# Six places in a quad for a router's choice, and the first gather moved beside the last quad

## What is computed

```
x = x + tanh(g_xattn) * attention(layernorm(x), ctx, mask)      # one head, 77 keys
n = layernorm(x)
probs = softmax(n @ gate_w.T)                                   # 8 experts
g, m = top_k(probs.transpose, k=512)                            # per batch and expert
h = gelu(n[m] @ w1) @ w2                                        # 512 -> 2048 -> 512
x = x + tanh(g_ffn) * scatter_add(g * h)
```

## Time and profile before

| | us |
|---|---|
| median of 3 runs | 1548.4 (1545.95 to 1549.63) |
| the profiled execution | 1545.97, its span 1543.9 |
| TensorE busy | 1493.0 (97%) |
| VectorE, ScalarE, GpSimd busy | 1012.3, 721.4, 587.7 |
| first hidden product of expert 0 starts | 172.19 |
| first output product starts | 180.67 |

### The profile page before, as it was taken

The page is one execution under the profiler, slowest core; times in us unless marked ns, Lnnn a source line. Parts: engine busy times, 40 slices in busy tenths (PEclk is TensorE's granted clock), DMA queues, the critical chain, the costliest instruction groups (busy, mean ns, idle before and its releaser), DMA issues.

```text
span 1543.9 us, 20288 instructions
## 1 busy us (share of the span) xinstructions
PE 1493.0 (97%) x7329; PEld 1226.4 (79%) x7329; DVE 1012.3 (66%) x1716; ACT 721.4 (47%) x1270; POOL 587.7 (38%) x552
## 2 busy tenths in 40 slices
PE   6987899999999999999999999999999999999997
PEld 6755577888788888888888888888888888888886
DVE  2687776557866667676757676667667675766543
ACT  2244433455444454454445544445445444554532
POOL 2264655525434135314443244413541444323311
PEclk9999799999999999999999999999999999999999
DMA  7274633533324333244323432333324433442133
GB/s 232 77 241 157 216 103 116 138 120 92 109 83 89 102 83 115 64 102 103 105 87 82 110 110 83 82 101 91 108 70 96 110 94 98 82 110 82 42 76 76
DMA packets 101385, 163.37 MB, mean 106 GB/s; under 512 B 7411, under 2 KB 45315, under 8 KB 101285
## 3 DMA queue, kind: packets, MB, share of 16 engines
q1 hardware_dynamic: 86885, 128.50, 26.3%
q0 software_dynamic: 14400, 33.56, 11.6%
HBM read 128.48 MB, written 33.55 MB: 105 GB/s over the span
## 4 chain that ended last, share of the span: by engine, by line
PE 90%; DVE 6%; DMA 1%; ACT 1%; issue 1%; POOL 0%; SPq 0%; POOLq 0%; DVEq 0%
PE bank L1410 43%; PE bank L1296 34%; PE bank L1272 4%; PE bank L1587 2%; PE bank L565 1%; PE bank L589 1%; DVE atleast L972 1%; DMA x_s<-in_x 1%; DVE onehot L1470 1%; DVE x L839 1%; PE bank L406 1%; PE bank L1459 0%; DMA ctx_raw<-in_ctx 0%; PE bank L554 0%; PE bank L582 0%
## 5 line engine op out<-in xcount | busy, mean ns | idle before, releaser
L1410 PE MATMUL bank<-w2hl,hh 128*128 128x512 f32 x2024 | 628.6, 392 | 0.4 <-DVE hid_low L1288 0.4
L1296 PE MATMUL bank<-xo,whl 128*128 128x512 f32 x2352 | 541.8, 389 | 1.9 <-DVE mix L1360 1.9
L1296 PEld LDWEIGHTS bank<-xo,whl 128*128 128x128 f32 x2352 | 441.4, 188 | 94.4 <-DVE mix L1360 2.3
L1410 PEld LDWEIGHTS bank<-w2hl,hh 128*128 128x128 f32 x2024 | 375.9, 188 | 75.8 <-DVE hid_low L1288 0.8
L1410 PE MATMUL bank<-w2hl,hid_low 128*128 128x512 f32 x1012 | 394.0, 389 | 0.0
L1410 PEld LDWEIGHTS bank<-w2hl,hid_low 128*128 128x128 f32 x1012 | 190.0, 188 | 39.7
L1534 POOL DMA_INDIRECT layer_out<-y,slot_row x64 | 104.6, 1635 | 294.6 <-ACT y L1449 279.3
L1226 POOL TENSOR_TENSOR whl<-raw,whl 128x512 fp32r<-128x512 f32 x56 | 81.3, 1451 | 259.5 <-ACT whl L1189 259.5
L1257 DVE TENSOR_TENSOR w2hl<-raw,w2hl 128x512 fp32r<-128x512 f32 x213 | 146.0, 707 | 38.5 <-ACT w2hl L1252 38.5
L1252 ACT ACTIVATE w2hl<-raw 128x512 fp32r<-128x512 f32 x228 | 136.5, 624 | 63.4 <-DMA raw<-in_L_ffn_w 39.5
L1231 POOL TENSOR_TENSOR whl<-wsum,whl 128x512 fp32r<-128x512 f32 x56 | 73.9, 1320 | 183.5 <-ACT whl L1210 183.5
(11 more groups left out here) (231 smaller groups left out, 1783.9 us busy)
## 6 DMA issues: line engine op xcount, KB each, us to landing
raw<-in_L_ffn_w SPq DMA_DIRECT2D x228, 256.0 KB
raw<-in_L_ffn_w SPq DMA_DIRECT2D x72, 512.0 KB
x_s<-in_x SPq DMA_DIRECT2D x8, 1024.0 KB, 9.2
layer_out<-x SPq DMA_DIRECT2D x8, 1024.0 KB, 10.4
xn_rows<-xn SPq DMA_DIRECT2D x8, 1024.0 KB, 5.2
raw_k<-in_L_xattn_Wk SPq DMA_DIRECT2D x1, 1024.0 KB, 5.4
raw_q<-in_L_xattn_Wq SPq DMA_DIRECT2D x1, 1024.0 KB, 11.0
raw_v<-in_L_xattn_Wv SPq DMA_DIRECT2D x1, 1024.0 KB, 13.2
```

Of the source, the lines that this page charges most:

```text
L1296: last = pe.matmul(bk[:, :], whl[:, p % 2, part, 2 * w + k, :], xo[:, xpart, x, k, :], start=(not adds and k == 0 and part == HIGH and xpa ...
L1410: last = pe.matmul(Y_BANKS[c][:, :], high if hpart == HIGH else low[:, c * P:(c + 1) * P], w2hl[:, f % 4, part, :], start=(s == 0 and hpar ...
```

## The change

- A quad has six places in place of five (`PLACES`), and piece 0 is at place 2 of quad 4 (`FIRST_PLACE`), at the same point of that quad as before. On TensorE place 0 is now ahead of `route`, and place 1, which is new, behind the second weighing; on VectorE place 0 is where it was and place 1 stands between `router_in` and `weights_in`. Quad 5 so has pieces 4 to 9, quad 6 has 10 and 11 ahead of its weighings, the one-hots (12) ahead of `weigh` 2 on VectorE with the slots' product ahead of weighing 3 on TensorE, and the slots (13) ahead of `weigh` 3. Quad 7 has none.
- In quad 7 TensorE turns two blocks of gathered tokens ahead of weighing 3 and the other two behind it. VectorE's low part of w1 moves from behind quad 7 to ahead of its `weights_in`, and all four low parts of tokens stand ahead of the two last `logits_out` (before, the fourth stood behind them).
- ScalarE does the squares of the quad before (`square_x1`) ahead of `exps` in quads 5 and 6; in quad 7 all four stand behind `e_out`. The tokens' high parts stand ahead of the last quad's squares.
- GpSimd does, for quads 4 and 5, all four rows ahead of `first_deviations` of the quad after the next, and the gather stands ahead of the `deviations` of quad 6.

```diff
@@ -537,7 +537,7 @@
         VG_BANK, CHOICE_BANK = bank[5], bank[7]
 
 
-        CHOOSE_FROM, PLACES = QB, 5
+        CHOOSE_FROM, PLACES, FIRST_PLACE = QB, 6, 2
 
         def turn_bank(turn):
             return bank[T_BANKS[turn_at[turn] % 2]]
@@ -606,21 +606,28 @@
                 turn_e(pe, q)
                 if q + 1 < NQ:
                     score(pe, q + 1, Q - 1)
+                between(q, 0)
                 if q == 0:
                     wait_evacuated(pe, len(steps) - 1)
                 route(pe, q)
-                between(q, 0)
-                for i in range(Q - 1):
+                for i in range(2):
                     weigh_pe(pe, q, i)
                 between(q, 1)
+                weigh_pe(pe, q, 2)
+                between(q, 2)
+                if q == NQ - 1:
+                    for c in range(2):
+                        tokens_pe(pe, 0, c)
                 weigh_pe(pe, q, Q - 1)
-                between(q, 2)
+                between(q, 3)
                 for i in range(Q):
                     if q + 2 < NQ:
                         turn_x(pe, q + 2, i)
                     if i == 1:
-                        between(q, 3)
-                between(q, 4)
+                        between(q, 4)
+                between(q, 5)
+            for c in range(2, NC):
+                tokens_pe(pe, 0, c)
 
         def attention_act(act):
             def square(q, i):
@@ -673,14 +680,15 @@
             for q in range(NQ):
                 if q == NQ - 1:
                     w1_high_act(act, 0, 0, 0)
-                    for i in range(2):
+                elif q - 1 >= LATE:
+                    for i in range(Q):
                         square_x1(q - 1, i)
                 exps(q)
                 e_out(q)
                 if q == CHOOSE_FROM:
                     choice_act(act, 0)
-                if q - 1 >= LATE:
-                    for i in range(2 if q == NQ - 1 else 0, Q):
+                if q == NQ - 1:
+                    for i in range(Q):
                         square_x1(q - 1, i)
                 if LEAD <= q + 1 < NQ:
                     for i in range(Q):
@@ -688,6 +696,9 @@
                 if q + 2 < NQ:
                     for i in range(Q):
                         x_out(q + 2, i)
+
+            for c in range(NC):
+                first_tokens_act(act, c)
             for i in range(Q):
                 square_x1(NQ - 1, i)
 
@@ -761,14 +772,16 @@
                 if q >= 0:
                     deviations(q)
                     for i in range(Q):
-                        if i == Q // 2:
+                        if i == Q // 2 and q < LATE:
                             first_deviations(it + 1)
                         rows(q, i)
-
-
-            deviations(NQ - 2)
+                    if q >= LATE:
+                        first_deviations(it + 1)
+
+
             for c in range(NC):
                 gather_pool(pool, 0, 0, c)
+            deviations(NQ - 2)
             deviations(NQ - 1)
             for f in range(2):
                 w2_low_sub(pool, 0, 0, f)
@@ -865,16 +878,17 @@
             prep_out(dve, prep_dve, False, 1, own)
             for q in range(NQ):
                 softmax_in(q)
-                if q == NQ - 1:
-                    between(q, 0)
                 if q >= 2 and q - 2 != CHOOSE_FROM - 1:
                     logits_out(q - 2)
                 if 1 <= q <= LATE:
                     stats(q - 1, range(Q))
                     moments(q - 1)
+                between(q, 0)
                 if q + 1 < NQ:
-                    between(q, 0)
                     router_in(q + 1)
+                else:
+                    w1_low_part(dve, 0, 0, 0)
+                between(q, 1)
                 weights_in(q)
                 weigh(q, 0)
                 if q == CHOOSE_FROM:
@@ -883,22 +897,20 @@
                 weigh(q, 1)
                 if q == NQ - 1:
                     mean_out(q, slice(0, Q // 2))
-                between(q, 1)
+                between(q, 2)
                 weigh(q, 2)
-                between(q, 2)
+                between(q, 3)
                 weigh(q, 3)
                 if q == NQ - 1:
                     mean_out(q, slice(Q // 2, Q))
                 elif q >= LATE:
                     mean_out(q)
-                between(q, 3)
                 between(q, 4)
-            w1_low_part(dve, 0, 0, 0)
-            for c in range(NC - 1):
+                between(q, 5)
+            for c in range(NC):
                 split_tokens_dve(dve, 0, c)
             logits_out(NQ - 2)
             logits_out(NQ - 1)
-            split_tokens_dve(dve, 0, NC - 1)
 
         def attention_over(eng):
 
@@ -1051,11 +1063,8 @@
         def beside_attention(do):
 
             def between(q, place):
-                at = (q - CHOOSE_FROM) * PLACES + place - 1
-                if q == NQ - 1:
-                    for piece in ((N_PIECES, N_PIECES + 1) if place == 0 else ()):
-                        do(piece)
-                elif 0 <= at < N_PIECES:
+                at = (q - CHOOSE_FROM) * PLACES + place - FIRST_PLACE
+                if 0 <= at < N_PIECES + 2:
                     do(at)
             return between
 
@@ -1985,8 +1994,6 @@
             prep_out(act, prep_act, True, 0)
             attention_act(act)
 
-            for c in range(NC):
-                first_tokens_act(act, c)
             for f in range(2):
                 w2_high_act(act, 0, 0, f)
             w1_high_act(act, 0, 0, 1)
@@ -2034,8 +2041,6 @@
         def _(pe):
             prep_pe(pe, 0)
             attention_pe(pe, beside_attention(first_choice_pe(pe)))
-            for c in range(NC):
-                tokens_pe(pe, 0, c)
             hidden_pe(pe, 0, 0)
 
             pe.wait_ge(rinv_ready, NQ)
```

## The result

The change costs a little: 1552.98 us (median of 19 runs, 1550.74 to 1555.73) against 1548.4 us (19 runs, 1545.95 to 1553.97), a ratio of 1.0028 (95% interval 1.0020 to 1.0035). The profiled execution took 1551.53 us, with a span of 1549.5 us against 1543.9. TensorE's mean granted clock over the runs was 0.9863 of full speed, against 0.9887 in the runs of the kernel before that stand beside experiments 1 to 8.

What follows compares the result with a forecast made beforehand. TensorE, busy 1493.0 of 1543.9 us, was taken as the bound. 0 (quads 5, 6) + 0.6 (quad 7) - 0.2 (squares to output) + 2.4 (clock) - 0.3 = +2.5 on 1548.4, so 1550.9 us; range 1544.5 to 1554.

Steps and rivals of the forecast that it cites:

- rival B: Quad 6: clock falls before 151 us, so slots and weighing 3 run at half clock; +3.8, 1552.2 us; chance 0.16.
- Part 1: Quads 5 and 6: six places and an earlier choice, VectorE's added work balanced by filled waits; 0 us.
- hot comparison: VectorE's large comparison for the one-hots, now in quad 6: 2.28 us, forecast to end near 150 us.
- Part 2: Quad 7: two token blocks turned ahead of weighing 3, +1.0, less 0.4 for the slots' product; last weighing 0.6 us later.
- rival C: Quad 7: gathered tokens land late and hold weighing 3; at 2 us late, 1552.9 us; chance 0.07.
- Rival D: Quad 7: the pause is cut in two, so the clock stays at 2.4 GHz; 1544.5 us; chance 0.14.
- Part 3: From quad 7's last weighing through squares, logits and choice to output: -0.2 us, between -0.9 and +0.6.
- Rival E: Before output: the hidden products are the bound and start 2.6 us earlier, no clock penalty; 1545.8 us; chance 0.10.
- Part 4: Before output: TensorE waits 4 to 6 us, so output products start at 1.2 GHz; 2.35 us, bounds 0 and 3.0.
- the 0.3 wait: TensorE's wait of 0.3 us for a count of the second choice, forecast to go away.
- Rival A: At output start: the clock holds, so no 2.4 us cost; time given as 1548.6 us; chance 0.13.

Runs made afterwards that it cites:

- experiments 1 to 8: Follow-up kernels, some editing the changed kernel and some the kernel before; their medians run from 1548.88 to 1557.45 us.
- experiment 7: Changed kernel plus extra products that nobody reads, in TensorE's pauses in quad 6 and before output; 1549.11 us, 1.0005 of the kernel before.
- experiment 5: Kernel before with only the six places and the earlier choice; gather, tokens and the ScalarE and GpSimd orders unchanged; 1549.56 us, 1.0009.
- experiment 10: Changed kernel with two of quad 7's squares ahead of the token copies, and unread products in pauses of quads 4 to 7 and before output; 1545.55 us, 0.9986.
- experiment 9: Changed kernel with two of quad 7's four squares ahead of ScalarE's token copies, two behind; 1551.83 us, 1.0013 of the kernel before.
- experiment 3: Changed kernel with all four squares of quad 7 ahead of ScalarE's token copies; 1557.45 us, 1.0057 of the kernel before.
- experiment 4: Changed kernel with all four token blocks turned behind quad 7's last weighing; 1555.18 us, 1.0046 of the kernel before.
- experiment 2: Changed kernel with one-hots and slots behind the last weighing of quad 6; 1554.21 us, 1.0033 of the kernel before.
- experiments 8 and 11: Kernel before plus unread products: six behind quad 6's last weighing (1550.53 us, 1.0009), or in its pauses from quad 4 to output (1550.77 us, 1.0021).

## Why the prediction was right in kind and short in size

The forecast was 1550.9 us, +2.5; it came to 1552.98, +4.6, inside the range and at the edge of the forecast's own 1549 to 1553. Direction and mechanism held: more room on TensorE, no less work in front of the output products, and a clock that falls in the new room. But what came is nearer to rival B (0.16, 1552.2 us), whose extra fall of the clock happened on top of the forecast's own. Of the signs that I had named, the clock and the wait at output came true; softmax of quad 7 was 2.0 us late and not within 0.5, output started at 183.59 and not between 180.5 and 182, and the hidden products started at 172.09, hardly earlier, because what comes ahead of them was 3.2 us late. (Two slips in the sums: A's time comes to 1548.5, and D with half of E to 0.19.)

- **Part 1, quads 5 and 6: 0 forecast, +2.0 in the profile.** This is the term that was mis-sized. The hot comparison ended at 151.0 and the gather went out at 153.9, 1.0 and 1.9 us behind the 150 and 152 of the forecast, and softmax of quad 7 moved from 153.21 to 155.24. I had taken 0.4 us for VectorE's wait for weighing 3 behind the slots' product, at the full clock. It ran at half: 2.06 us, a wait of 1.38. That is rival B, whose condition (a low clock before 151 us) was met. With the pauses of quad 6 filled (experiment 7) weighing 3 took 1.10 us, the wait was 0.43, as forecast, and softmax started at 154.15: the slow weighing is 1.1 of the 2.0 us. The other 0.9 lies ahead of the gate's logits of quad 6: softmax of quad 6 started at 137.94 against 137.30, and the logits were read at 147.12, against 145.19 in experiment 5. Four operations of the pick took 0.35, 0.77, 0.82 and 0.88 us beside GpSimd's rows, where before they took 0.81, 0.30, 0.34 and 0.52, 0.85 more in all; but in experiment 7 the last three took 0.30, 0.37 and 0.53, and the logits were read at 147.02 all the same. Experiment 5 says that the places alone can cost 0 at this mark, and 1.1 us in the median; it lacks the new orders on ScalarE and GpSimd.
- **Part 2, quad 7: +0.6 forecast, +1.1 measured.** The tokens were never late (rival C is out: there is no wait before L1552, though the last gather took 9.3 us). The eight transposes ahead of weighing 3 took 1.18 us, near the 1.04 of the sum. The -0.4 for the slots came (the weighings start 6.1 us behind softmax, 6.5 before), but weighing 2 now ran at the slow clock too, and VectorE read it 1.7 us behind weighing 1, against 1.0 before. Rival D is out for the kernel as it stands (0.50 from 150 to 166), though experiment 10 shows what it spoke of: transposes 0.66, router 1.06, eight weighings 3.18 and 1.02 us, 2.8 us less than in rows 3.
- **Part 3, squares to output: -0.2 forecast, -0.2 measured** (5.2 to 5.3 up to the logits, 9.1 to 8.8 from there). Experiment 9 shows the mechanism, experiment 3 its edge. Rival E is out: TensorE waited 5.75 us for the split hidden block.
- **Part 4, the clock at output: +2.1 forecast (2.4 less the 0.3 wait), +1.7 in the profile.** The pause was to be 4 to 6 us and was 5.75. Rival A is out: the window at 182 shows 0.50. The clock came back within 186 to 188, sooner than the 24 hidden products of rows 3 let me expect.

Counted over the whole, the clock is the larger part of the cost: with the pauses of quad 6 and before output filled, 3.9 of the 4.6 us were gone (experiment 7). It isn't all of the change's making, as 0.7 of the 3.4 us found at the marks come from quad 7, which ran at half clock before as well. The page of the Trainium skill that I had weighed ("TensorE: Matmul & The Clock Gate", "Part 1: The HAM clock gate") puts the ramp at under 1% of a typical kernel's span and advises against fitting it. The size agrees, as all that was measured here is 0.3% of the time; but most of that 0.3% was the ramp, so a comparison of two versions can't leave it out.

Left open: whether experiment 4 was slower than the change only by the fall of the clock that its profile shows ahead of the edit; what makes the 0.9 us of part 1 that lie ahead of quad 6's gate logits; and whether experiment 2's order would pay with the clock held.

## What to carry to other kernels

A pause on TensorE was paid twice here, once as the wait and once as the work behind it at 1.2 GHz, so a change that takes work out from under it has to say what fills the room; dead products are a cheap test of this, and here also the cure (0.9978 of the time before, 0.9963 to 0.9992). The same cure did nothing for the kernel before, because the next thing in line was a gather that now came just behind a 1 MB write: a cost taken away is worth what is late next, and it pays to look for it first. Where small two-input VectorE operations stand near long GpSimd ones, see in the timeline that they come first.

## What the chip showed that I had not expected

- Six VectorE products of 128x32 took 6.2 us in place of 1.1, the first four 1.01 to 1.33 us each beside GpSimd subtractions of 1.26 us (experiment 3).
- The last of four indirect gathers landed 4.1 to 4.4 us behind its issue when a 1 MB write to memory was issued 0.6 to 1.0 us behind it, and 7.9 and 8.0 us when the write was issued up to 0.2 us ahead of it (experiments 8 and 11). In the change, beside the write of quad 6's output, it took 9.3 us.
- A pause of 1.88 us before 401 us, the same in both kernels, was followed by a clock of 0.60 (402 to 404 us) in the profile after and by the full clock in the one before; the slow clock cost 1.3 us.
